# The first warm-up of TensorE: 96 fp32 products of 32x32 in place of 22 bf16 products of 128x128

## What is computed

```python
def basic_block(x, w1, w2, stride=1, ds=None):
    out = jax.nn.relu(conv3(x, w1, stride) * BN_S)
    out = conv3(out, w2, 1) * BN_S
    identity = conv1x1(x, ds, stride) * BN_S if ds is not None else x
    return jax.nn.relu(out + identity)
x = basic_block(x, e0b0c1, e0b0c2)
x = basic_block(x, e0b1c1, e0b1c2)
f0 = x
x = basic_block(x, e1b0c1, e1b0c2, stride=2, ds=e1b0ds)
x = basic_block(x, e1b1c1, e1b1c2)
f1 = x
x = basic_block(x, e2b0c1, e2b0c2, stride=2, ds=e2b0ds)
x = basic_block(x, e2b1c1, e2b1c2)
x = (jax.nn.relu(deconv2(x, dec0w) * BN_S) + f1) * BN_S
x = (jax.nn.relu(deconv2(x, dec1w) * BN_S) + f0) * BN_S
...
x = x + _L0_conv_ref(_gn(x), ...)
```

## Time and profile before

| what | us |
|---|---|
| median of 2 runs | 89.31 |
| lowest and highest of them | 88.95, 89.67 |
| the profiled execution, its own time | 89.11 |
| its span, first to last instruction | 87.3 |
| TensorE busy in the span | 79.6 (91%) |
| VectorE, ScalarE, GpSimd busy | 55.2, 43.7, 25.6 |

### The profile page before, as it was taken

One profiled execution on the slowest core, in us unless ns is written; L12 is line 12 of the kernel. 1 busy time (PEld: TensorE's weight loads), 2 busy tenths in 40 slices (PEclk: granted clock), 3 DMA queues, 4 the chain that ended last, 5 costly groups with the idle time before them and its releaser, 6 DMA issues.

```text
span 87.3 us, 1463 instructions
## 1 busy us (share of the span) xinstructions
PE 79.6 (91%) x510; PEld 71.5 (82%) x510; DVE 55.2 (63%) x164; ACT 43.7 (50%) x94; POOL 25.6 (29%) x39
## 2 busy tenths in 40 slices
PE   5976999999999999999999999999999999998700
PEld 3765999998777889999988777999999999775500
DVE  5678999799968696422223658899656767212640
ACT  6007015679455056555521149799999995000400
POOL 7200051899950000444451000100389000000230
PEclk9999999999999999999999999999999999999996
DMA  1978920024684106540000000000000000000085
GB/s 26 260 203 302 323 118 0 0 84 92 161 239 155 30 0 195 167 126 0 0 0 0 0 0 4 0 0 0 8 0 0 0 0 0 0 0 0 8 275 209
DMA packets 4183, 6.51 MB, mean 75 GB/s; under 512 B 464, under 2 KB 2128, under 8 KB 4176
## 3 DMA queue, kind: packets, MB, share of 16 engines
q1 hardware_dynamic: 4032, 6.29, 23.4%
q10 hardware_dynamic: 144, 0.13, 0.4%
HBM read 5.37 MB, written 1.05 MB: 74 GB/s over the span
## 4 chain that ended last, share of the span: by engine, by line
PE 83%; DMA 5%; DVE 3%; SPq 2%; issue 1%; ACT 1%; DVEq 0%
PE psum L830 80%; DMA raw<-e0b0c_in 5%; DVE result L821 2%; SPq L443 1%; PE psum L866 1%; PE psum L1010 1%; PE psum L873 1%; ACT w_e0b0c L519 1%; PE psum L1057 1%; SPq L447 0%; DVEq L175 0%; DVE last L747 0%; DVE up L813 0%; PE psum L857 0%; PE psum L850 0%
## 5 line engine op out<-in xcount | busy, mean ns | idle before, releaser
L495 POOL TENSOR_TENSOR odd<-relu,odd 128x363 fp32r<-128x363 f32 x12 | 13.6, 1149 | 15.4 <-ACT odd L560 15.4
L830 PE MATMUL psum<-shared,w_e0b0c 128*128 128x364 f32 x72 | 12.5, 332 | 0.7 <-ACT w_e0b0c L519 0.7
L830 PEld LDWEIGHTS psum<-shared,w_e0b0c 128*128 128x128 f32 x72 | 11.9, 188 | 1.0 <-issue 0.9
L760 DVE SCALAR_TENSOR_TENSOR relu<-psum,inside 128x363 f32<-128x363 f32 (+1 forms) x16 | 8.1, 510 | 6.6 <-PE psum L830 5.1
L830 PE MATMUL psum<-shared,w_e0b1c 128*128 128x364 f32 x72 | 12.2, 329 | 0.0
L830 PEld LDWEIGHTS psum<-shared,w_e0b1c 128*128 128x128 f32 x72 | 12.1, 188 | 0.1
L830 PE MATMUL psum<-odd,w_e0b0c 128*128 128x512 f32 x48 | 11.6, 400 | 0.0
L830 PE MATMUL psum<-odd,w_e0b1c 128*128 128x512 f32 x48 | 11.6, 400 | 0.0
L830 PEld LDWEIGHTS psum<-odd,w_e0b0c 128*128 128x128 f32 x48 | 9.1, 189 | 2.2
L830 PEld LDWEIGHTS psum<-odd,w_e0b1c 128*128 128x128 f32 x48 | 9.0, 189 | 2.2
L560 ACT ACTIVATE odd<-relu 128x363 fp32r<-128x363 f32 x12 | 6.1, 506 | 7.2 <-DVE relu L760 7.2
(11 more groups left out here) (122 smaller groups left out, 125.6 us busy)
## 6 DMA issues: line engine op xcount, KB each, us to landing
x_sb<-x_in SPq DMA_DIRECT2D x4, 160.0 KB, 3.8
raw<-e0b0c_in SPq DMA_DIRECT2D x2, 256.0 KB, 4.9
raw<-e0b1c_in SPq DMA_DIRECT2D x2, 256.0 KB, 5.0
raw<-e1b1c_in SPq DMA_DIRECT2D x2, 256.0 KB, 3.3
raw<-e2b1c_in SPq DMA_DIRECT2D x2, 256.0 KB, 2.8
raw<-e1b0c_in SPq DMA_DIRECT2D x1, 448.0 KB, 4.0
raw<-e2b0c_in SPq DMA_DIRECT2D x1, 448.0 KB, 4.0
x_sb<-x_in SPq DMA_DIRECT2D x2, 192.0 KB, 3.9
```

The lines of the kernel that those rows point to most:

```text
L495: pool.tensor_tensor(split_of(piece, 1), fp32_of(piece), split_of(piece, 0).bitcast(F32), ALU.subtract).then_inc(lo_ready, 1)
L760: last = dve.scalar_tensor_tensor(out=target, in0=sums, scalar=0.0, in1=mask, op0=ALU.max, op1=ALU.mult)
L830: last = pe.matmul(target, w, moving, start=(first and n == 0), stop=(final and n == len(terms) - 1), skip_group_check=skip)
```

## The change

TensorE's first warm-up gets another form: in each of six rounds one fp32 product for each of the 4 x 4 combinations of 32 rows (`of_r`, of weights and moving operand) and 32 columns (`of_c`, the output's partitions), with 256 moving columns. Products of row group r write bank r. A new fp32 tile of zeros, 128x256, is set by VectorE between `zeros` and `quad_mask`, ahead of `ground_set`. The second warm-up and all others stay as they were.

```diff
-WARM_UP = [22, 14]
+WARM_UP = [6, 14]
...
         zeros = sb("zeros", [P, BANK // 2], BF16)
+        zeros_fp32 = sb("zeros_fp32", [P, BANK // 2])
...
             dve.memset(zeros[:], 0.0)
+            dve.memset(zeros_fp32[:], 0.0)
             dve.memset(quad_mask, 0.0)
             dve.memset(eps4[:], 4.0 * GN_EPS).then_inc(ground_set, 1)
...
+            def warm_up_tiles(rounds):
+
+                for t in range(rounds):
+                    for r, c in itertools.product(range(4), range(4)):
+                        of_r, of_c = slice(CH * r, CH * r + CH), slice(CH * c, CH * c + CH)
+                        pe.matmul(psum[of_c, r, 0:256], zeros_fp32[of_r, 0:CH], zeros_fp32[of_r, 0:256],
+                                  start=(t == 0), stop=(t == rounds - 1), skip_group_check=True)
...
             pe.wait_ge(ground_set, 1)
-            warm_up(WARM_UP[0])
+            warm_up_tiles(WARM_UP[0])
             sum_stats(0)
             warm_up(WARM_UP[1])
```

More of the change, by code:

```diff
@@ L24 @@
+import itertools
 from contextlib import ExitStack
```

## The result

The median went from 89.31 us (88.95 to 89.67, 2 runs) to 90.73 us (90.42 to 91.05, 2 runs): ratio 1.0148, 95% interval 1.0097 to 1.0200. So it is slower by 0.8 to 1.4 us; the two intervals only just overlap. The comparisons leave out executions more than 1.5% above the fastest of their kernel; where that could hide the effect itself, all times are given.

The account below looks back on a forecast made before the run. Bound: the first weights' transfer, ScalarE's conversion, then TensorE from 8.08 us. Memset 0, removed products 0, added tiles 0 to 0.2 us gave 89.1 to 89.3 for the profiled execution; forecast 89.4 against the median, range 88.8 to 91.5.

Parts of the forecast that it names:

- The bound and the slack: Before TensorE's start at 8.08 us: statistics up to about 0.3 us later cost nothing, beyond that a microsecond each.
- The memset: Added 128x256 fp32 memset on VectorE: about 0.27 us, shifts what follows by about 0.21 us, cost 0.
- Sixteen tiles side by side: First warm-up: a round costs one product, end at 5.15 us, 5.3 with the tail; 0 to 0.2 us.
- Rival 1: First warm-up: column tiles of a row group wait for one another; 91.5 (chance 0.09), with no overlap 96.7 (0.05).
- The clock: TensorE at the start: 1.2 GHz until some 3.7 us, 2.4 GHz from then on.
- Rival 3: The clock does not rise on the tile products: 90.0 to 92, in the middle 90.7; chance 0.09.
- The fetch: TensorE's added instructions bring the first fetch some 9 us earlier, around 8.5 us, after the weights landed: 0.
- rival 4: A 16 KB instruction packet before 7.3 us holds back the first weights: +1 us, 90.4; chance 0.03.
- L: Theory of the experiments: the warm-up is too long, and the statistics product behind it is late.
- Issue of the instructions: First warm-up: 192 pairs at 0.030 us a pair are 5.8 us, end at 7.1; real rate somewhere below.
- Rival 2: Issue limits the first warm-up: 0.030 us a pair, end 7.1, +1.4 us, 90.7; chance 0.11.
- The change of shape: TensorE going between tile shapes: the change itself costs nothing visible.

Follow-up runs that it names:

- e1b_four_rounds_again: The changed kernel with four rounds of tiles in place of six, run once more for a second profile: 89.47 us.
- e5_two_wide: The changed kernel with two rounds of tiles with 512 columns in place of six with 256: 89.13 us, ratio 0.9968.
- e9_const_by_act: e5_two_wide with the transfer of `same_channel` issued by ScalarE instead of SP: 89.45 us, ratio 1.0006.
- thin tiles: The changed kernel with 32 moving columns in place of 256, the same 96 products: 91.41 us, ratio 1.0208.

## Why the prediction came out as it did

The forecast was no change (89.4), the range up to 91.5. The time fell into the range, the likeliest case did not come true. That the range held is in part luck: its upper part was built from rivals 1 to 4, of which only the fourth occurred, and the round that costs more than its passes, which made most of the lateness, was not among them. By its steps:

*The bound and the slack: right for the profile that it was read from.* 0.29 us of slack at VectorE's rows, then a microsecond for a microsecond. The long bf16 warm-up shows it (2.55 us late, 2.2 us lost). But the slack is of one execution, as the second look at the kernel before shows: with the weights landed 0.35 us earlier and the clock risen later, VectorE's rows were the last there.

*The memset: right.* 0.27 us, the first product 0.28 us later (1.35), the statistics of x at 3.86 where they were at 3.74; nothing of it reached the end.

*Sixteen tiles side by side: right for the tiles, wrong for the round.* Rival 1 is out. In the changed kernel, line 867 in 1.34 to 1.5 us, then in 4.65 to 5.0 and in 5.75 to 6.4 us:

```profile
L867 PE MATMUL psum<-zeros_fp x16: 627/630/632, 1.3 to 1.5; 32*32 32x256 f32 x16
...
L867 PE MATMUL psum<-zeros_fp x29: 546/628/629, 4.0 to 5.0; 32*32 32x256 f32 x29
...
L867 PE MATMUL psum<-zeros_fp x47: 374/396/398, 5.4 to 6.4; 32*32 32x256 f32 x47
```

Sixteen first passes start in the first 0.15 us, four column tiles of each row group among them, each with its own weight load. The sentence of the Trainium skill that a weight load overlaps a matmul in flight only across row groups ("TensorE: Matmul & The Clock Gate", "The mechanism") does not hold here, and this measurement decides. But a round costs more than its two passes. Two profiles have their tiles at the low clock to the end: four rounds of 256 columns take 4.53 us, two of 512 take 4.09 us (the first block is of e1b_four_rounds_again, the second of e5_two_wide; e9_const_by_act has 4.09 too):

```profile
1.35 4.53 PE L867 MATMUL psum<-zeros_fp 32*32 32x256 f32 x128 [1.35 <-DVE eps L680]
```

```profile
1.61 4.09 PE L867 MATMUL psum<-zeros_fp 32*32 32x512 f32 x64 [1.61 <-DVE eps L680]
L867 PE MATMUL psum<-zeros_fp x64: 1052/1056/1057, 1.6 to 4.6; 32*32 32x512 f32 x64
```

The columns are the same, 16 times 1024 in two passes, and the two rounds more cost 0.44 us: 0.22 us a round beside the passes. The thin tiles say nearly the same: 6 rounds of 2 x 0.053 us of columns take 2.21 us, some 0.35 a round. The weight loads show where this time lies. In the profile of two rounds the first load of the second round starts at 3.32 us, as the first tile's two passes end, and the next one only at 3.55 (line 867 in 3.3 to 3.54 us, then to 3.56):

```profile
L867 PEld LDWEIGHTS psum<-zeros_fp x1: 168/168/168, 3.3 to 3.3; 32*32 32x32 f32 x1
L867 PEld LDWEIGHTS psum<-zeros_fp x2: 123/146/168, 3.3 to 3.6; 32*32 32x32 f32 x2
```

So a round of 256 columns is 0.86 + 0.22 = 1.08 us at the low level, not 0.86. bf16 tiles have nothing of it (0.21 us a round). The Trainium skill's span model ("TensorE: Matmul & The Clock Gate", "Measured speedup vs the span model": one product's duration and some 4 ns for each further tile) agrees with the trace for the first bf16 round, whose 16 starts lie within 0.06 us. The 16 first passes of fp32 take 0.11 us to start, 7 ns a tile, and of what lies between two rounds the model says nothing. **This is the term that was mis-sized**: "If all sixteen tiles run side by side as the four row groups do, a round costs one product". Why the second load waits was not tried.

*The clock: the rest.* I took the rise at 3.7 us from one profile as if it were the kernel's. In the changed kernel the products still have 628 ns at 4.65 to 5.0 us and fall to 396 by about 5.3 us; in its second profile the fall is at 4.4, and in the kernel before it was at 3.7 once and at about 6 the other time. With rounds of 1.08 us and 0.62 at the high level (an estimate that fits both profiles), a rise at 3.75 gives 1.35 + 2.4 + 3.8 x 0.62 + 0.17 = 6.3 us, a rise at 5.3 gives 1.35 + 3.95 + 2.35 x 0.62 + 0.17 = 6.9, against 7.0 measured. So of the 1.7 us between the 5.3 us that I forecast and the 7.0, 1.0 us is the size of the round and the rest is when the clock rose. Rival 3 as it stands is out: in all eight profiles with fp32 tiles of 256 or 512 columns the duration of the warm-up's products falls by a third before the first real product. What I had wrong is to take one time of the rise as given. It lies between 4.4 and 7.8 us in these eight, and at 3.7, about 6 and 6.2 us in the three with bf16 products of the whole array; that the tiles raise it later is not shown by these.

*The fetch: rival 4, given 0.03, is there.* The step that failed is "In the first case the first fetch comes some 9 us earlier, around 8.5 us, after the weights have landed: 0". The packet came at 6.4. In the fourteen profiles it ran at 3.9 (thin tiles), 4.6 (bf16 tiles), 5.8 to 6.7 (256-column fp32 tiles), 9.7, 11.9 and 12.1 (512 columns) and 17.7 to 18.2 us (whole array): it comes the sooner, the more instructions TensorE has behind it. With both passes of an fp32 product counted, the seven packets before 7 us run 1.6 to 2.7 us after the 190th weight load or matmul of the trace; for the later ones the distance is anything from -1.4 to 3.3 us, so this count is no rule. The price of +1 us was a little low where the packet struck: in the five profiles with 256-column fp32 tiles the first weights landed at 8.59 to 9.11 us in four and at 7.01 in one. In the six profiles with no packet before 9 us in which SP issued them at the same place, they landed at 6.80 to 7.36. In the changed kernel it lies beside L, and adds 0.2 us in one profile and 0.4 in the other.

*Issue of the instructions: no limit.* 16 pairs in 0.15 us are at most 10 ns each. Rival 2 is out. The change of shape costs nothing that can be seen: the statistics product starts behind the last tiles without an idle time, and the equal 60.5 us show that nothing later is slower.

## What to carry to other kernels

A filler that keeps an engine warm stands in a queue, so it must end before the wait behind it does, at the low clock and not at the one of a lucky profile; move the instruction that others wait for ahead of the last part of the filler, as six of ten executions here show, or make the filler from few long instructions. Count the instructions as well as the time: many small ones pull a fetch of 16 KB forward, and if it falls among the first transfers, any of them can be a microsecond late. Price a new shape with a short and a long variant of it, since what a round costs beside its columns shows in no neighbour's row.

## What the runs showed of the hardware that I had not expected

- A round of sixteen fp32 tiles of 32x32 costs 0.22 us beside its two passes at the low clock, one of bf16 tiles nothing that can be seen: 0.21 us for 256 columns, as for one whole-array product of the same columns.
- The clock rises at a time that changes from execution to execution, with the same instructions before it: about 3.7 and about 6 us in two profiles of the kernel before, and about 7.8 us at the latest where the warm-up had no long idle time. Where TensorE idled for 2.8 to 4.2 us after a short warm-up, it had not risen when the first real products began, 9.6 to 10.1 us into the span.
- One instruction packet of 16 KB (0.95 to 1.2 us of one of the 16 DMA engines) goes with a transfer of 64 or 256 KB that lands 1.2 to 1.8 us later than in the kernel before, in six profiles, and with none in a seventh; none of the seven profiles with the packet after 9 us has such a delay (the most is 0.7 us). Which engine it meets, and how much of the transfer is left there, I take for the difference; it was argued, not shown.
